# Asking for the shared block's weights one event later: SyncE waits for TensorE to pass a jump as well as for the last contraction

## What is computed

```python
def _L0_gnn_ref(x_nodes, x_edges, path_coeffs, src, dst, path_indices):
    x1 = x_nodes[src].reshape(-1, N_SEG, EXTENT)
    x2 = x_edges.reshape(-1, N_SEG, EXTENT)
    contrib = path_coeffs[None, :, None] * x1[:, i1, :] * x2[:, i2, :]
    edge_out = jnp.zeros(...).at[:, i3, :].add(contrib)
    return jnp.zeros(...).at[dst].add(edge_out.reshape(-1, OP_SIZE))
...
def _L0_ffn_ref(hidden_states, Wr, sWg, sWu, sWd, Wg, Wu, Wd):
    for e in range(NS):                       # NS = 2 shared blocks
        shared = shared + _swiglu_ffn(x, sWg[e], sWu[e], sWd[e])
    probs = softmax(x @ Wr); top_w, top_i = top_k(probs, 6)
    for e in range(E):                        # E = 64 experts
        routed = routed + _swiglu_ffn(x, Wg[e], Wu[e], Wd[e]) * gate[:, e:e + 1]
    return shared + routed + x
x = x + _L0_gnn_ref(_layernorm(x), edge_attr_512, path_coeffs, src, dst, path_indices)
x = x + _L0_ffn_ref(_layernorm(x), Wr, sWg, sWu, sWd, Wg, Wu, Wd)
```

## Time and profile before

| | |
|---|---|
| median of 3 runs | 1060.63 us (1059.23 to 1063.25) |
| the profiled execution | 1064.09 us, span 1062.9 us |
| mean granted TensorE clock | 0.974 |
| TensorE multiplications busy | 881.1 us (83%) |
| VectorE busy | 562.9 us (53%) |
| mean transfer rate over the span | 302 GB/s |

### The profile page before, as it was taken

How to read it: one execution, slowest core, us unless ns; L and a number is a source line. 1 busy time by engine, 2 the same in 40 slices (tenths; PEclk the granted TensorE clock), 3 DMA queues, 4 the chain that set the end, 5 groups by cost and what they waited for, 6 DMA issues and landing times.

```text
span 1062.9 us, 20671 instructions
## 1 busy us (share of the span) xinstructions
PE 881.1 (83%) x7145; PEld 477.0 (45%) x7146; DVE 562.9 (53%) x1321; ACT 226.3 (21%) x580; POOL 349.8 (33%) x390
## 2 busy tenths in 40 slices
PE   0267777677677677899999999999997999989988
PEld 0033333333334334485454544646444445445455
DVE  6499999999999999576211121121211221211116
ACT  1032232232233231241211111111210211211100
POOL 4654434434534520022322332333232232332120
PEclk9999899999999999999999999999998999999999
DMA  7857657657657654666999999999999999999928
GB/s 230 331 198 233 212 197 238 206 196 242 200 198 244 200 200 160 260 247 231 385 396 394 393 389 395 390 393 388 397 394 407 382 392 396 398 395 388 393 75 323
DMA packets 70374, 321.10 MB, mean 302 GB/s; under 512 B 12908, under 2 KB 13061, under 8 KB 48344
## 3 DMA queue, kind: packets, MB, share of 16 engines
q1 hardware_dynamic: 48050, 260.82, 64.5%
q0 software_dynamic: 21248, 56.55, 16.3%
q10 hardware_dynamic: 934, 1.80, 0.6%
HBM read 308.55 MB, written 13.62 MB: 303 GB/s over the span
## 4 chain that ended last, share of the span: by engine, by line
PE 57%; DVE 18%; issue 12%; DVEq 9%; DMA 2%; ACT 0%; ACTq 0%; another core or an unknown queue 0%
PE ps L1262 21%; DVE big L611 15%; PE ps L1320 11%; PE ps L875 7%; DVEq L609 4%; DVEq L602 4%; PE ps L1197 4%; PE ps L630 3%; PE ps L902 3%; PE ps L1294 2%; PE ps L1255 2%; DMA pair_d<-big 1%; PE ps L1314 1%; DVEq L611 1%; DMA big<-in_dst 1%
## 5 line engine op out<-in xcount | busy, mean ns | idle before, releaser
L611 DVE TENSOR_TENSOR big<-big 128x512 f32 (+1 forms) x640 | 385.0, 677 | 17.5 <-DMA big<-xn_d,idx 14.9
L630 PE MATMUL ps<-big,mixed 128*32 128x256 f32 x2512 | 171.8, 414 | 133.2 <-DVE big L611 120.7
L1262 PE MATMUL ps<-big 128*64 128x512 f32 x1024 | 237.0, 605 | 17.4 <-issue 16.4
L339 POOL DMA_INDIRECT big<-xn_d,idx x157 | 169.5, 1079 | 200.0 <-DVE big L611 144.7
L1154 POOL DMA_INDIRECT big<-h_d,idx x64 | 63.1, 986 | 361.6 <-issue 277.6
L630 PEld LDWEIGHTS ps<-big,mixed 128*32 128x32 f32 x2512 | 80.0, 116 | 227.5 <-DVE big L611 139.2
L1272 DVE TENSOR_TENSOR mixed<-big,ps 128x256 f32<-128x256 f32 x64 | 27.0, 422 | 268.9 <-ACT big L1269 268.5
L1262 PEld LDWEIGHTS ps<-big 128*64 128x64 f32 x1024 | 68.8, 138 | 142.4 <-issue 139.9
L1320 PE MATMUL ps<-big,mixed 128*64 128x256 f32 x1024 | 124.6, 385 | 0.1
L1223 POOL DMA_INDIRECT y_d<-big,sia x74 | 75.4, 1020 | 118.8 <-DVE big L1333 60.5
L1320 PEld LDWEIGHTS ps<-big,mixed 128*64 128x64 f32 x1024 | 67.9, 136 | 34.3 <-issue 2.9
(11 more groups left out here) (213 smaller groups left out, 653.0 us busy)
## 6 DMA issues: line engine op xcount, KB each, us to landing
big<-in_L_ffn_Wg SPq DMA_DIRECT2D x64, 1024.0 KB
big<-in_L_ffn_Wu SPq DMA_DIRECT2D x64, 1024.0 KB
big<-in_L_ffn_Wd SPq DMA_DIRECT2D x64, 1024.0 KB
big<-in_edge_attr SPq DMA_DIRECT2D x39, 1024.0 KB
big<-y_d SPq DMA_DIRECT2D x10, 768.0 KB, 11.8
big<-xn_d,idx POOLq DMA_INDIRECT x157
big<-in_L_ffn_sWg SPq DMA_DIRECT2D x2, 1024.0 KB, 5.1
big<-in_L_ffn_sWu SPq DMA_DIRECT2D x2, 1024.0 KB, 7.2
```

Of the source, the lines that this page charges most:

```text
L339: pool.indirect_dma_start(xs[s][:, c, :], None, xn_d[:, :], bass.IndirectOffsetOnAxis(ap=table[:, c0 + c:c0 + c + 1], axis=0)).then_inc(x_ ...
L611: ins = dve.tensor_tensor(pr[k % 2][:, 0:chunks, EXT * p:EXT * (p + 1)], xs[s][:, 0:chunks, ds(o1, EXT)], es[s][:, 0:chunks, ds(o2, EXT)], ...
L630: ins = pe.matmul(edge_bank(k // 2)[WIN * h:WIN * (h + 1), h0:h0 + HP * EXT], onehot[s][:, CW * h + r, :], pr[k % 2][:, CW * h + r, :], st ...
L1262: ins = pe.matmul(bank(k2)[TA * h:TA * (h + 1), :].rearrange("p (w f) -> p w f", w=2), xgT[k2][:, k, 0:TA], gu[:, :, k, W * h:W * (h + 1)] ...
```

## The change

A new semaphore `past_extra` is counted up by a no-operation in TensorE's program, which stands directly behind the jump over the further items (and behind all multiplications of the graph part in program order). SyncE now waits for it as well as for `part_used` before it asks for shared block 0 and all that follows.

```diff
@@ -815,7 +815,10 @@
             pool.dma_start(none[s][k:k + 1, :], src[0:4].unsqueeze(0)).then_inc(y_out[s], 16)
 
 
+    past_extra = sem("past_extra")
+    pe.nop().then_inc(past_extra, 1)
     sync.wait_ge(part_used, nparts)
+    sync.wait_ge(past_extra, 1)
     shw = [load_shared(0, *shared)]
     load_expert(2, 2)
 
```

## The result

The changed kernel took 1070.01 us (median of 6 runs, 1068.97 to 1071.45) against 1061.14 us before (6 runs, 1059.23 to 1064.46): a ratio of 1.008, 95% interval 1.0064 to 1.0097, or 8.9 us slower. The forecast was 1066.5, or 5.9 us slower than the median it started from, so the direction and the range held and the size was 3 us short. Its profiled execution took 1070.96 us, span 1069.8.

A forecast was written before the change was run, and what follows sets the result against it. The weight stream sets the pace at the end and starts with the first item; 4.05 + 1.5 + 0.3 = 5.85 us on the median of 1060.63 gave 1066.5 us, range 1062.0 to 1070.5.

The forecast's parts named there:

- The likeliest case: TensorE's jump shortens to near 3.7 us; 1064.5 to 1068.5 us, chance 0.66.
- the second case: TensorE's jump keeps its 6.7 us, the turning is 7.0 us late; +9.5, 1070.1 us, chance 0.14.
- The jump: On TensorE's sequencer at 435.8, taken as waiting for code: 3.7 us in place of 6.701, bounds 0.06 and 6.7.
- The landing: Shared weights, first issued at 439.6 behind the nop, land at 451.2; the turning starts at 451.3.
- +4.05: Delay in us of the turning of H, from 447.24 to 451.3, by the late shared weights.
- The translation: Whatever moves the first item moves stream and TensorE; the expert part from there on keeps its length.
- the stream absorbed: Rival: TensorE's gaps behind 800 us shrink by the first items' lateness; 1061 to 1062 us, chance 0.08.
- +1.5 us: Clock's cost behind TensorE's 5.7 us wait ahead of the turning, half clock for about 3 us; bounds 0 and 1.8.
- this gives nothing: The faster jump brings L916 forward by 1.3 us without gain, since the turning waits for something later.
- The gather: First gather, moved from 461.54 to 467.0, meets the later stream's last backlog: +0.3 us, bounds 0 and 2.7.
- holding up nothing: The store of H, queued behind expert 2, lands near 462 and delays no other work.

The follow-up runs named there:

- e12: Changed kernel with SyncE's wait for the jump moved behind the shared block's three transfers, so only expert 2 and what follows waits; ratio 1.0005 to the kernel before.
- e4: Changed kernel with the semaphore count ahead of TensorE's jump in place of behind it; ratio 1.0032 to the kernel before.
- e11: Kernel e7 with the semaphore count ahead of the jump in place of behind it; ratio 1.0026 to the kernel before.
- e6: Kernel before without the four multiplications that nobody reads, every transfer up to the store of H at its old time; ratio 1.0052 to the kernel before.
- e3: Changed kernel with the four multiplications that nobody reads behind the wait for the shared weights, not ahead; ratio 1.0076 to the kernel before.
- e7: Changed kernel with TensorE's shared-weights wait moved behind the routing and six multiplications that nobody reads in place of four; ratio 1.0077 to the kernel before.
- e1: Changed kernel with TensorE's wait for the shared weights moved from ahead of the turning to behind the router products; ratio 1.0066 to the kernel before.
- e9: Changed kernel, unchanged, run again for a second trace; ratio 1.0082 to the kernel before.
- e2: Changed kernel with twelve multiplications that nobody reads in place of four; ratio 1.0065 to the kernel before.
- e10: Kernel e7 with expert 2 asked for behind the store of H in place of ahead of it; ratio 1.0046 to the kernel before.
- e8: Kernel before with only TensorE's wait for the shared weights moved ahead of the shared block's first part; ratio 1.0011 to the kernel before.
- e5: Kernel before, unchanged, run once more for a second trace; one run, 1064.91 us.

## Why the prediction was right, and where its size was off

**The range: held, in part by luck.** The likeliest case had 1064.5 to 1068.5 us, and 1070.01 lies outside it. It lies within the whole range, which reached to 1070.5 because it took in the second case, a jump that keeps its 6.7 us (1070.1 us). That case did not happen: its time was met by another route, the clock.

**The jump: right.** 3.46 us against my 3.7. Five traces in which the weights were asked for some 4.5 us ahead of it have 6.08 to 6.70 us, nine others 3.42 to 3.86. The second case, an unchanged jump, is ruled out for this kernel. What I drew from the taking of turns between queues in the Trainium skill (DMA: Bandwidth & Descriptors, Queues, rings and completion order) gave the wrong side: a backlog in another queue did cost the jump some 2.8 us (the mean of the five less that of the nine). Shown is that it depends on a backlog that stood before the jump (e12) and not on traffic that begins with it (e4, e11). That it is the fetch of code stays an inference, and the packets narrow it down. Each of the fourteen traces has a packet of 8 KB on the queue that the profile names `q14 instruction`, which starts 1.7 to 2.2 us after the jump starts, whether the jump is short or long. The short jumps end 1.2 to 2.1 us after that start and the long ones 4.3 to 5.0. So that packet isn't held up behind the weights; what the backlog lengthens comes after its start, and no trace here names it.

**The landing: right.** I put 11.8 us between the nop and the turning; it was 11.4 (436.3 to 447.73). The whole term, "+4.05", measured 3.5: counted from the start of L679, the turning begins at 15.05 us in place of 11.52. Against the 10.5 us of the traces in which L679 ran at full clock it is 4.6.

**The translation: right.** I said that nothing behind the first item makes its lateness good. The rest of the span is 592.0 us before and 592.2 after, and the gap of 7.48 us is there again with 7.43. Over all fourteen traces the rest is 589.8 to 592.8 us, on average 591.8 in the five in which the weights were asked for early and 591.2 in the nine others, so if the stream absorbed anything it was less than this scatter.

**The clock: the term that was mis-sized.** "+1.5 us", with a bound of 1.8, measured 6.2 (26.26 less 20.03). I took its price from the wait in the expert part, where the clock was back 3 us after work resumed. Here it was back only 15 us behind the start of the turning. e6 shows the same price without a late weight: 26.57 us from turning to product. In e3 the multiplications of L919 (128x512) stood at this very place, and the clock was back 3.7 us after they began. The turnings and router products ran at full clock throughout where they began with it (e3, e7), but behind a fall they ran long at half: the clock was back 14 to 16 us from the start of the turning in the traces of the changed kernel, e1, e4 and e6, each time 1.9 to 4.0 us after the shared block's first multiplications (L878, L875 in e6) had begun, and after 7 us, within the router products, in e9. It is the row of the nearest duration that I took, and not that of the nearest work.

**L916: "this gives nothing" holds for the start of the turning, not for the clock.** L916 is there to hold the clock, and its place depends on the jump ahead of it. In the changed kernel TensorE idled 6.95 us and not 5.7, since L916 (L919 there) ended at 440.78. Once the turning no longer waits for the weights (e1), it ends 2.4 us ahead of the layer norm, and the clock was lost; e7 fills that gap and kept the clock over the routing.

**The gather: right in the changed kernel, whose slow routing hid its cost.** TensorE has no wait at L1200 there: the gather starts at 468.26, when the transfer engines are idle. Once the wait and the clock are mended (e7), the same late queue costs 5.3 us of waiting at L1200 and 2.6 us more in the first product, far beyond the 2.7 that I had as a bound. There the store of `H`, which I had put down as holding up nothing, releases the gather. So the late weights cost 7 to 8 us by the ratios (5 to 8 by the medians) in any of these forms (e1, e2, e3, e7). The turning's wait, the half clock and the late gather lie over each other, and mending one or two of them returned at most 1.5 thousandths, which is within the intervals. Asking earlier returned more (e4, e11), and by its trace so did putting less ahead of the store of `H` (e10).

Measured size: in place of my 4.05 + 1.5 + 0.3 the traces have 3.5 for the turning, 6.2 for the clock and nothing for the gather. That is the whole 9.8 by which they differ, counted from the start of L679. The medians differ by 8.9.

**What stays open:** why the clock came back after 10 us in e9 and after 17 in the changed kernel's first trace, why it fell after 2.43 us of idleness in e1 and not in e8, and by what path a standing backlog lengthens the jump. No kernel here beats the kernel before; e8 and e12 are even with it.

## What to carry to other kernels

A transfer that is early by 4.5 us has that much slack and no more, and what stands behind it in the same queue has a slack of its own: look for the last user of each (here the first gather, 26 us on) before delaying the first. When work ahead of a wait shrinks, ask what kept the clock up until then, and take the clock's price from a row whose work after the fall is like yours. If two or three waits lie over each other, taking one away shows nothing: take them away together before calling a cause refuted.

## What the runs showed of the hardware that I had not expected

TensorE's far jump took 3.4 to 3.9 us with nothing asked for ahead of it and 6.1 to 6.7 us behind a backlog, while ScalarE's, GpSimd's and SyncE's took 45 to 58 ns at the same place. A no-operation with a semaphore count runs on TensorE's sequencer while the array works: in the changed kernel at 436.3, with L679 on the array until 437.24. Half clock lasted 17 us in the changed kernel, and for the last 15 of them TensorE was busy without a gap. The clock fell after waits of very different lengths: at 468.1 in e2, 0.7 us after one of 0.97 us had ended (the next product took 6.14 us), and after 2.15, 2.43, 2.50 and 2.61 us in e4, e1, e12 and e5, while it held through 2.43 us in e8. In the traces of before and e4 it was at half over most of L679, behind waits of 1.23 and 0.69 us.
